# A delta-rule attention phase: layer-norm roots moved to ScalarE, gate finishing on GpSimd, one k unit and the last v taps moved in their queues, the last inverse level interleaved

## The reference, cut to what matters

```python
q = silu(causal_conv(x @ Wq)); k = silu(causal_conv(x @ Wk)) * D ** -0.5; v = silu(causal_conv(x @ Wv))
alpha = sigmoid(x @ Wa + ba); beta = sigmoid(x @ Wb + bb)
def step(St, (q_, k_, v_, a_, b_)):          # for each of 512 tokens, 16 heads of 128
    err = St @ k_ - v_
    Sn = a_ * St - b_ * outer(err, k_)
    return Sn, Sn @ q_
o = scan(step, 0, ...)
o = (o - mean(o)) * rsqrt(var(o) + 1e-5) * ln_w + ln_b      # over each head's 128
return (o * sigmoid(x @ Wg)) @ Wo
```

## Time and profile before

| what | value |
| --- | --- |
| median of 3 runs | 3017.93 us |
| the profiled execution, its own time | 3018.13 us |
| its span, first to last instruction | 3016.3 us |
| PE busy | 2824.9 us (94%) |
| DVE busy | 1837.2 us (61%) |
| ACT busy | 1206.1 us (40%) |
| POOL busy | 611.9 us (20%) |
| mean granted TensorE clock | 0.969 |

### The profile page before, as it was taken

How to read it: one execution, slowest core, us unless ns; L and a number is a source line. 1 busy time by engine, 2 the same in 40 slices (tenths; PEclk the granted TensorE clock), 3 DMA queues, 4 the chain that set the end, 5 groups by cost and what they waited for, 6 DMA issues and landing times. The chain is left out here.

```text
span 3016.3 us, 37740 instructions
## 1 busy us (share of the span) xinstructions
PE 2824.9 (94%) x13038; PEld 1584.4 (53%) x13039; DVE 1837.2 (61%) x4645; ACT 1206.1 (40%) x2214; POOL 611.9 (20%) x669
## 2 busy tenths in 40 slices
PE   6999989989999968999999999999999999999787
PEld 3444434445665444666556665566655665554232
DVE  5767752011111557877787778877778777547586
ACT  4545521012212354444554445544454445422232
POOL 1111201301110403033321333123330233200000
PEclk9999989999999978999999999999999999999899
DMA  3100151031211821002101021000111001226213
GB/s 126 47 15 28 42 199 78 22 125 63 69 63 56 322 104 68 29 20 80 53 33 43 15 71 64 36 29 30 71 57 43 29 29 67 86 93 233 70 46 98
DMA packets 78423, 215.22 MB, mean 71 GB/s; under 512 B 12065, under 2 KB 12977, under 8 KB 69681
## 3 DMA queue, kind: packets, MB, share of 16 engines
q1 hardware_dynamic: 57472, 165.79, 15.2%
q0 software_dynamic: 9264, 28.36, 2.9%
q10 hardware_dynamic: 11520, 18.92, 1.7%
HBM read 156.25 MB, written 56.79 MB: 71 GB/s over the span
## 5 line engine op out<-in xcount | busy, mean ns | idle before, releaser
L2281 DVE SCALAR_TENSOR_TENSOR c_conv<-c_ps_pj,c_conv_t,c_conv 128x511 f32<-128x511 f32 (+2 forms) x495 | 368.0, 746 | 85.6 <-ACT c_conv L2119 74.0
L1812 POOL TENSOR_SCALAR c_gate<-c_gate 128x512 f32<-128x512 f32 x64 | 40.8, 638 | 934.3 <-ACT c_gate L2111 934.3
L1903 PE MATMUL c_ps_pj<-c_w_g,c_xs 128*128 128x512 f32 x512 | 227.7, 592 | 0.0
L1886 PE MATMUL c_ps_pj<-c_xs,c_w_v 128*128 128x512 f32 x480 | 225.8, 593 | 0.0
L1886 PE MATMUL c_ps_pj<-c_xs,c_w_k 128*128 128x512 f32 x480 | 217.9, 597 | 6.1 <-DMA c_xs<-xt_d 6.1
L1886 PE MATMUL c_ps_pj<-c_xs,c_w_q 128*128 128x512 f32 x360 | 195.1, 677 | 0.3
L2119 ACT ACTIVATE c_conv<-c_ps_pj,c_conv_t 128x512 f32<-128x512 f32 x165 | 127.8, 774 | 87.8 <-PE c_ps_pj L1886 85.8
L2300 DVE TENSOR_TENSOR c_block_X<-c_block_X,c_block_t 128x126 f32<-128x126 f32 (+22 forms) x496 | 143.5, 289 | 17.0
L2296 DVE TENSOR_TENSOR c_block_t<-c_block_L,c_block_X 128x126 f32<-128x126 f32 (+22 forms) x496 | 138.6, 279 | 17.0
L1903 PEld LDWEIGHTS c_ps_pj<-c_w_g,c_xs 128*128 128x128 f32 x512 | 93.6, 190 | 100.0 <-issue 100.0
L2171 ACT ACTIVATE c_err<-c_negL 32x128 f32<-32x128 f32 x256 | 78.6, 307 | 153.1 <-DVE c_negL L2365 148.3
(11 more groups left out here) (518 smaller groups left out, 5817.8 us busy)
## 6 DMA issues: line engine op xcount, KB each, us to landing
c_G<-cum_d SPq DMA_DIRECT2D x16, 1024.0 KB, 4.7
c_xs<-xt_d SPq DMA_DIRECT2D x16, 1024.0 KB, 4.8
ot_d<-c_oT ACTq DMA_DIRECT2D x64, 256.0 KB, 2.0
b_w_gu<-in_w_gu SPq DMA_DIRECT2D x8, 1408.0 KB, 20.8
y_slots<-x_y SPq DMA_DIRECT2D x40, 256.0 KB, 2.0
a_x<-in_x SPq DMA_DIRECT2D x8, 1024.0 KB, 6.3
d_x<-x SPq DMA_DIRECT2D x32, 256.0 KB, 2.9
d_switch<-in_switch_w SPq DMA_DIRECT2D x4, 2048.0 KB, 17.1
```

The lines of the kernel that those rows point to most:

```text
L1886: mm = e.matmul(bank_of[xb][u][:, :], w["kqv"[u // HG]][:, k, (u % HG) * DH:(u % HG + 1) * DH], xs[xb][:, k, :], start=(k == 0), stop=(k = ...
L1903: mm = e.matmul(pj[(xb + i) % 2][:, :], xs[xb][:, k, i * P:(i + 1) * P], w["g"][:, k, :], start=(k == 0), stop=(k == KD - 1))
L2281: e.scalar_tensor_tensor(oc, bank_of[buf][u][:, 0:SEQ - s], conv_t[buf][:, m, h, TAPS - 1 - s:TAPS - s], oc, ALU.mult, ALU.add).then_inc(c ...
```

## The change

* **Roots on ScalarE.** `norm_guess` and `norm_refine` (15 small DVE instructions a round) are gone. ACT computes `exp(-0.5 * ln(var + eps))` in two instructions (`norm_root`), after its tap of chunk 1. The activation table of the chunk stage is now the one that has both functions. `norm_offset` moves to chunk 3. In the tail ACT does the same.
* **Gates finished later.** POOL waits for `T_turned` before `finish_gates`, in every round, and so before `bias_gains` in round 0 too.
* **Unit 3 in another bank.** It goes to `r_ps`, which r_blocks writes later; r_blocks now waits for unit 3's taps. Unit 6 waits for a gate copy instead of unit 3's taps.
* **Unit 5's taps later.** ACT makes the first tap behind the copies of Z, DVE the others behind its copy of R.
* **First inverse level.** Steps 0 and 1 (one column) and step 30 (one row) of the 31 are one `scalar_tensor_tensor` each instead of a product and a sum.
* **Last v taps.** DVE does the taps of unit 11 behind the first kd of the next round instead of at the end of its own.
* **Last inverse level interleaved.** Unit 7's second half is cut into two single k steps. The order is z_half(0), k step, z_half(1) and r_half(0) matmul by matmul in turn, k step, r_half(1). Before it was z_half(0), z_half(1), r_half(0), r_half(1), half unit.

```diff
-    SUB_STEPS = 1 + 1 + 2 * (BB - 1)
+    SUB_STEPS = 1 + 1 + 2 * (BB - 1) - 3
-    RSTD_STEPS = 16
+    RSTD_STEPS = 3
...
             bank_of[s][HG + 1] = kq_ps
+            bank_of[s][HG - 1] = r_ps
...
             def a_round(r, buf, last=False):
+                e.wait_ge(T_turned, r + 1)
                 finish_gates(r, buf)
                 if after_first(r):
-                    e.wait_ge(T_turned, r + 1)
...
-                        if u in (HG - 1, HG) and gates_before:
-                            e.wait_ge(g_copied, TPB * (q - 1) + u)
+                        if u == HG - 1:
+                            e.wait_ge(kd_done, (TPB - 1) * q)
+                        elif u == HG:
+                            e.wait_ge(g_copied, TPB * q)
                         elif u == HG + 1:
-                            if gates_before:
-                                e.wait_ge(A_done, TPB * q)
-                        elif u in (HG + 2, HG + 3):
+                            e.wait_ge(A_done, TPB * q)
+                        elif u == HG + 2:
+                            e.wait_ge(g_copied, TPB * q - 1)
+                        elif u == HG + 3:
                             e.wait_ge(conv_step, TAP_STEPS * (CONVS * q + u))
...
                     e.wait_ge(zl_done, 4 * r + 2)
+                    if not last:
+                        e.wait_ge(conv_step, TAP_STEPS * (CONVS * (r + 1) + HG + 2))
...
-                for p in range(PAIRS):
-                    z_half(p)
-                for p in range(PAIRS):
-                    r_half(p)
-                next_unit(HG + 3, (1,))
+                for i in range(2 * HG):
+                    z_half(0, i)
+                next_quarter(HG + 3, 2)
+                for i in range(2 * HG):
+                    z_half(1, i)
+                    r_half(0, i)
+                next_quarter(HG + 3, 3)
+                for i in range(2 * HG):
+                    r_half(1, i)
...
+            def norm_root(q):
+                step = q * RSTD_STEPS
+                e.wait_ge(o_mean, NM * q + NM)
+                e.activation(o_ve[:, :], o_mv[:, :, 1], ACT.Ln, bias=con["eps"][:, :]).then_inc(o_rstd, 1)
+                e.wait_ge(o_rstd, step + 1)
+                e.activation(o_rs[:, :], o_ve[:, :], ACT.Exp, scale=-0.5).then_inc(o_rstd, 1)
...
-                e.preload_act_table_set("exp_and_others")
+                e.preload_act_table_set("natural_log_exp_and_others")
...
                     if c < TPB - 1:
                         next_tap(c)
+                    if c == 1 and after_first(r):
+                        norm_root(r - 1)
...
                 next_tap(HG)
-                next_tap(HG + 1)
...
                     e.activation(Z[down, :, :, up], z_block[b][down], ACT.Copy).then_inc(zl_done, 1)
+                next_tap(HG + 1)
...
+                    if k == 1:
+                        e.scalar_tensor_tensor(below[:, :, 0], left, top, below[:, :, 0], ALU.mult, ALU.add).then_inc(sub_step, 1)
+                    if n == 1:
+                        e.scalar_tensor_tensor(below[:, 0, :], top, left, below[:, 0, :], ALU.mult, ALU.add).then_inc(sub_step, 1)
...
                     if after_first(r):
+                        if c == 0:
+                            taps(r, buf, CONVS - 1, None)
                         norm_part(r - 1, c)
...
-                for u in range(HG - 1, HG + 2):
+                for u in range(HG - 1, HG + 1):
                     next_taps(u)
                 e.wait_ge(rl_ready, 4 * r + 1)
                 e.tensor_copy(R[even_of[0], :, :, odd_of[0]], r_block[0][even_of[0]]).then_inc(rl_done, 1)
+                next_taps(HG + 1)
                 next_taps(HG + 2)
...
                 norm_stats(r, TPB - 1)
-                next_taps(CONVS - 1)
```

More of the change, by code:

```diff
@@ L1635, in phase_delta @@
         o_st, o_mv = sb("o_st", [P, NM, 6]), sb("o_mv", [P, NM, 2])
-        o_ve, o_t, o_rs, o_nb = sb("o_ve", [P, NM]), sb("o_t", [P, NM]), sb("o_rs", [P, NM]), sb("o_nb", [P, NM])
+        o_ve, o_rs, o_nb = sb("o_ve", [P, NM]), sb("o_rs", [P, NM]), sb("o_nb", [P, NM])
         corners = err[:, :, :].rearrange("p h m -> p (h m)").rearrange("p (c h j) -> p c h j", c=TPB, h=HG)
@@ L1866, in _, with unit @@
         def _(e):
-            def unit(q, xb, u, halves_=(0, 1), xs_at=None, gates_before=True):
+            def unit(q, xb, u, halves_=(0, 1), xs_at=None, ks=None):
                 for half in halves_:
@@ L1884, in unit @@
                             e.wait_ge(conv_step, TAP_STEPS * (CONVS * q + u + 1))
-                    for k in range(half * KD // 2, (half + 1) * KD // 2):
+                    for k in ks or range(half * KD // 2, (half + 1) * KD // 2):
                         mm = e.matmul(bank_of[xb][u][:, :], w["kqv"[u // HG]][:, k, (u % HG) * DH:(u % HG + 1) * DH], xs[xb][:, k, :],
                                       start=(k == 0), stop=(k == KD - 1))
-                mm.then_inc(pj_ready, 1) if halves_[-1] == 1 else None
+                mm.then_inc(pj_ready, 1) if k == KD - 1 else None
             def gate_piece(r, xb, i, last):
@@ L2016, in turn_inverse, with next_quarter, z_half, r_half @@
                     mm.then_inc(tl_ready, 1)
[L2018 to L2032, removed]
+                def next_quarter(u, k):
+                    if not last:
+                        unit(r + 1, 1 - buf, u, (k // 2,), 16 * half + 16, ks=(k,))
+                        return
+                    h = (u + 1) * HG + k
+                    out_part(h // NH, (h % NH,))
+                def z_half(p, i):
+                    c, h = 2 * p + i // HG, i % HG
+                    if i == 0:
+                        e.wait_ge(tl_done, PAIRS * r + p + 1)
+                    mm = e.matmul(z_pair[p][lower_half, c % 2, h, :], negL[upper_half, c, h, lower_half],
+                                  T[upper_half, c, h, upper_half], start=True, stop=True)
+                    if i == 2 * HG - 1:
+                        mm.then_inc(zl_ready, 1)
+                def r_half(p, i):
+                    c, h = 2 * p + i // HG, i % HG
+                    if i == 0:
+                        e.wait_ge(zl_done, 4 * r + 3 + p)
+                    mm = e.matmul(r_pair[p][upper_half, c % 2, h, :], Z[lower_half, c, h, upper_half],
+                                  R[lower_half, c, h, lower_half], start=True, stop=True)
+                    if i == 2 * HG - 1:
+                        mm.then_inc(rl_ready, 1)
                 for u in range(HG, HG + 2):
@@ L2245, in tail @@
                 a_round(r, buf, None, last=True)
+                e.preload_act_table_set("natural_log_exp_and_others")
+                norm_root(r)
                 for c in range(TPB):
@@ L2291, in diagonal_inverse @@
                 e.transpose(block_L[:, :, :], mats(corners[:, :, :, :]).unsqueeze(2).to_broadcast([P, BB, 2, NM])).then_inc(sub_step, 1)
+                made = step + 2
                 for i in range(BB - 1):
                     n, k = BB - 1 - i, i // 2 + 1
-                    t = block_t[:, 0:n * k].rearrange("p (j k) -> p j k", k=k)
[L2295 to L2299, removed]
+                    left, top, below = block_L[:, i + 1:BB, i], block_X[:, i, 0:k], block_X[:, i + 1:BB, 0:k]
+                    e.wait_ge(sub_step, made)
+                    if k == 1:
+                        e.scalar_tensor_tensor(below[:, :, 0], left, top, below[:, :, 0], ALU.mult, ALU.add).then_inc(sub_step, 1)
+                        made += 1
+                        continue
+                    if n == 1:
+                        e.scalar_tensor_tensor(below[:, 0, :], top, left, below[:, 0, :], ALU.mult, ALU.add).then_inc(sub_step, 1)
+                        made += 1
+                        continue
+                    t = block_t[:, 0:n * k].rearrange("p (j k) -> p j k", k=k)
+                    e.tensor_tensor(t, left.unsqueeze(2).to_broadcast([P, n, k]), top.unsqueeze(1).to_broadcast([P, n, k]),
+                                    ALU.mult).then_inc(sub_step, 1)
+                    e.wait_ge(sub_step, made + 1)
                     e.tensor_tensor(below, below, t, ALU.add).then_inc(sub_step, 1)
+                    made += 2
                 e.wait_ge(sub_step, step + SUB_STEPS)
@@ L2351, in norm_part @@
                     norm_mean(q)
-                elif c == 1:
-                    norm_guess(q)
-                    norm_refine(q, (0,))
-                elif c == 2:
-                    norm_refine(q, (1, 2))
+                elif c == TPB - 1:
                     norm_offset(q)
```

21 lines of the change are left out of this document (removed).

## The result

The changed kernel takes **2970.43 us** (median of 4 runs, 2966.34 to 2971.98); the kernel before took 3017.51 in the same comparison (4 runs). The ratio is 0.9844, 95% interval 0.9827 to 0.9861: 1.6% faster. The forecast was 2964, range 2948 to 2986.

The account below looks back on a forecast made before the run. The prediction took TensorE, busy 94% of the span, as the bound. Rounds 1 to 14 at 3.0 us (42), round 0 (11), round 15 (0.8) and tail (0.3) gave 54 off 3018.1: 2964 us, range 2948 to 2986.

Parts of the forecast that it names:

- the halves side by side: Last inverse level: z_half(1) and r_half(0) run together instead of one after the other, 0.8 us less a round.
- PE 1.35 late behind the chunk stage: Chunk stage, steady rounds: the moved last v taps delay negL of chunk 1, so PE starts chunk 2 1.35 us later.
- The inverse 2.0 shorter: First inverse level on DVE: 0.7 us from single instructions and 1.3 from the gates' move, 2.0 together.
- The 1.3 of collisions: First inverse level: four DVE block products slowed beside POOL's gates, 1.3 us together a round, avoided by moving the gates.
- ACT's tap of unit 5 out of T's way: Before z_blocks: T's spread started 0.36 us after DVE's last turn because ACT was on this tap, now moved.
- The wait for T gone: z_blocks, rounds 1 to 14: PE's 2.03 us wait vanishes with 0.6 to spare; PE's waits together gain 0.7.
- The clock: Behind z_blocks, rounds 1 to 14: without the wait for T PE's clock stays up, 1.47 us gained a round.
- the rival with the new waits of chunks 1 and 2: Chunk stage: the new wait of 0.5 + 1.3 us still lowers the clock once a round; 2985 us, chance 0.12.
- Moved gates, new wait of r_blocks, ACT's queue before `turn_inverse`: From DVE's turn to `turn_inverse`: possible delays, at worst 0.3 us for the gates and 0.78 for ACT's tap; taken as nothing.
- The roots: Chunk stage: moving the fifteen root instructions off DVE gains nothing, since DVE waits for ACT's tap in their place.
- Round 0: Whole first round: 8.1 us of wait for T, 2 of low clock and 0.8 in the last inverse level go, 11 together.
- Round 15 and the tail: Kernel's end: 0.8 us gained in the last round, 0.3 in the tail where fifteen root instructions become two.

Follow-up runs that it names:

- e1: The changed kernel with DVE's taps of unit 11 put back at the end of the round; 2951.55 us, ratio 0.9780 to the kernel before.
- e3: The changed kernel with POOL's gates, and round 0's biases, again not held back by `T_turned`; 2990.71 us, ratio 0.9908 to the kernel before.
- e10: The changed kernel with product and sum as two instructions again in steps 0, 1 and 30 of the first inverse level; 2980.36 us, ratio 0.9858.
- e5: The kernel before with only the gates' move: POOL waits for `T_turned` before `finish_gates` and round 0's biases; 3007.92 us, ratio 0.9975.
- e11: The kernel before with only unit 5's taps moved (ACT: behind the copies of Z, DVE: behind its copy of R); 3022.30 us, ratio 0.9996.
- e9: The changed kernel with the inverse roots on DVE again, nothing else undone; 2982.10 us, ratio 0.9865 to the kernel before.
- e4: The changed kernel with the norm's means at chunk 1 instead of chunk 0 and ScalarE's roots behind the tap of unit 2; 2955.93 us, ratio 0.9796.

## Why the prediction held, and where it was off

The time lies in the range, and it does so by the mechanism that was forecast, not by luck: the wait for T and the low clock behind it are gone. One term, the halves side by side, came to a quarter of its size. The sum was 54 us; the span became 48.0 shorter, the median 47. By its steps, in round 6:

* **PE 1.35 late behind the chunk stage**: 20.88 - 19.53 = 1.35. Exact, and shown by e1 to be the moved taps. The forecast had it as a term of the sum, but did not say that this part alone makes the change 19 us worse than it could be.
* **The inverse 2.0 shorter**: 20.49 - 18.65 = 1.84. The 1.3 of collisions is shown by e3; the single instructions are 0.5, not 0.7 (e10).
* **ACT's tap of unit 5 out of T's way**: forecast as 0.36 of the sum, under the heading that DVE's queue is what is late for T. e5 and e11 show that both queues have to be freed. Behind the tap the wait is 2.03 whatever DVE does, and the gates' move alone gives nothing in a steady round; without the tap DVE alone still makes it 1.68.
* **The wait for T gone**: it is, in all steady rounds. Waits together -2.10 + 1.35 = -0.75, forecast 0.7.
* **The clock**: 1.62, forecast 1.47, as z_blocks itself ran partly at the low clock too. e3 (0.70) keeps the clock up, e11 (1.68) and e5 (2.03) do not: the rival with the new waits of chunks 1 and 2 did not come true.
* **Moved gates, new wait of r_blocks, ACT's queue before `turn_inverse`**: nothing forecast, nothing found; r_blocks to z_half is 6.09 against 6.10.
* **The roots**: forecast as no gain in the rounds. e9 shows 0.43 a round. The step charged DVE's 1.1 us of lateness at the inverse after the roots had left, and did not ask how late it would be with them.
* **The halves side by side, 0.8**: this is the term that was off. It came to 0.21. The mechanism was right (1.08 for both, 0.01 apart), but the step counted 0.96 "less a 0.1 for one more change between small and full tiles". A half is 0.93, and the new order has four more changes at 0.17. 0.59 x 16 rounds = 9 us of the sum.
* **Round 0**: forecast 11, and 10.6 by PE's starts. (The marks' 9.5 has the later chunk stage of round 1 in it.)
* **Round 15 and the tail**: forecast 0.8 + 0.3. PE starts round 15 at 2528.04 instead of 2575.54, 47.5 earlier, so 0.5 of the 48.0 is left for both.

The sum missed by 6: 9 too much for the interleaving, less what the clock gave more, 0.15 x 14 = 2. The rest is about 1 us a term or less.

## What to carry to other kernels

Read which queues a late result goes through and which of them is held up next: two moves that are worth 8 us and nothing alone were worth 50 together. An instruction moved into a waiting engine's gap is free only if nothing on the path stands behind it in that queue. The taps moved here bought 0.3 us before chunk 1 and cost 1.6 behind it. A wait of constant length is a sign to look for: what ends it may hang on the waiting engine's own earlier work, as here through the tap. If small matmuls are to run side by side, keep them in one block: each further change between tile sizes took back a fifth of what the pairing saved.

## What the runs showed of the hardware

* A change between 64x64 tiles and the full array cost 0.17 us on the mean (0.19 from small to full, 0.14 from full to small), from the starts in the changed kernel.
* A stop of PE cost 0.26 to 0.27 us more than the wait that the profile lists (changed kernel's chunk stage, e1, e4).
* A DVE product of two SBUF operands beside POOL's `tensor_scalar` took 0.56 instead of 0.22; taps with one operand in PSUM beside the same instruction took no longer (2.19 for three). Each of the 71 slow products of the kernel before ended 0.03 to 0.16 behind the POOL instruction that it had started under.
* Behind a wait of 1.68 us in the same place of the round the clock was 0.50, behind one of 0.70 it was 1.00. In e5, with 2.03, round 1 of the profiled execution stayed up, and it was 1.6 shorter than the others (93.98 against 95.58). Its ten runs lie between 3004.93, the profiled one, and 3013.43; that the count of low stretches makes this spread is not shown, since one execution has a trace.
* Two single `scalar_tensor_tensor` of 31 columns took 0.31 each from start to start; a `tensor_tensor` of the same size 0.24 (e10).
